# A four-layer graph network on one core: attention projections inside the attention passes, zero products, and a shorter path between passes

## The reference

```python
x = _layernorm(x + gcn(x, edge_weight))       # two convolutions with relu, then x @ Wfc + bfc
x = _layernorm(x + gat(x))                    # 8 heads
x = _layernorm(x + hgt(x, node_type, edge_type))
x = _layernorm(x + l3(x))

# gat, after its own layer norm and x @ W_in + b_in
e = leaky(scores_u[src] + scores_v[dst]); ex = exp(e - segment_max(e, dst)[dst])
agg = segment_sum(x[src] * ex, dst) / segment_sum(ex, dst)
out = agg @ W_ff + b_ff

# hgt: k, q, v by node type, kt and vt by edge type
e = (q[dst] * kt).sum(-1) * pri * scale; a = softmax of e over the edges of dst
agg = segment_sum(a * vt, dst)
out = relu(agg @ W_a[node_type] + x @ loop_weight + bias)   # W_a[type] = sum of 4 basis matrices, scaled

# l3
e = relu([h_src, h_dst] @ V.T + b) + h_src @ D.T + h_dst @ E.T; out = segment_sum(xw[dst] * scaler * e, src)
```

## Time and profile before

| | us |
|---|---|
| median of 3 runs | 7790.5 |
| the profiled execution | 7788.46 |
| its span | 7786.7 |
| PE busy in the span | 5059.6 (65%) |
| DVE busy | 4681.0 (60%) |
| ACT busy | 3283.5 (42%) |
| POOL busy | 4933.0 (63%) |
| indirect DMAs: sort, four passes, l3 | 784, 3328, 832 |
| data moved | 921.29 MB, 118 GB/s |

### The profile page before, as it was taken

One profiled execution on the slowest core, in us unless ns is written; L12 is line 12 of the kernel. 1 busy time (PEld: TensorE's weight loads), 2 busy tenths in 40 slices (PEclk: granted clock), 3 DMA queues, 4 the chain that ended last, 5 costly groups with the idle time before them and its releaser, 6 DMA issues. The chain is left out here.

```text
span 7786.7 us, 118192 instructions
## 1 busy us (share of the span) xinstructions
PE 5059.6 (65%) x26286; PEld 3803.4 (49%) x26287; DVE 4681.0 (60%) x12672; ACT 3283.5 (42%) x7820; POOL 4933.0 (63%) x4975
## 2 busy tenths in 40 slices
PE   6777775666665677772555557865666665777774
PEld 4555654444454555551444444435555543555553
DVE  7666664555554777774445545436666566566666
ACT  0222221444444455440444434435666541655553
POOL 0677775777776777774777770037777700777774
PEclk6666566888887888885666668977877777898897
DMA  0222221222223122233666672457777722666665
GB/s 27 59 53 54 55 55 46 54 55 55 55 55 47 53 55 54 55 52 90 179 180 179 182 164 85 143 169 221 234 225 229 216 69 80 208 201 200 201 200 139
DMA packets 818177, 921.29 MB, mean 118 GB/s; under 512 B 120930, under 2 KB 657002, under 8 KB 817706
## 3 DMA queue, kind: packets, MB, share of 16 engines
q0 software_dynamic: 198144, 441.54, 22.6%
q1 hardware_dynamic: 403498, 368.52, 15.9%
q10 hardware_dynamic: 216320, 109.07, 4.8%
HBM read 724.85 MB, written 193.87 MB: 118 GB/s over the span
## 5 line engine op out<-in xcount | busy, mean ns | idle before, releaser
L783 POOL DMA_INDIRECT arena<-t,stage_idx x3328 | 3268.1, 982 | 1249.8 <-issue 992.8
L822 PE MATMUL ps<-arena 128*128 128x128 f32 (+2 forms) x8320 | 1801.7, 378 | 770.0 <-DMA arena<-t,stage_idx 640.3
L822 PEld LDWEIGHTS ps<-arena 128*128 128x128 f32 x8320 | 1581.2, 258 | 1036.3 <-issue 935.6
L831 DVE TENSOR_TENSOR arena<-arena,ps 128x512 f32 (+2 forms) x1040 | 835.2, 803 | 733.0 <-PE ps L822 666.9
L739 POOL DMA_INDIRECT d_rec<-arena x784 | 782.5, 998 | 438.7 <-issue 241.5
L2664 POOL DMA_INDIRECT arena<-t,stage_idx x832 | 831.7, 1000 | 297.0 <-issue 224.2
L819 PE MATMUL ps<-int_tmp 128*128 128x512 bf16 (+1 forms) x1664 | 554.5, 402 | 622.9 <-DVE arena L831 340.3
L1861 PE MATMUL ps<-arena 128*128 x2496 | 393.4, 295 | 584.5 <-DVE arena L2087 323.5
L1263 PE MATMUL ps<-arena 128*128 128x416 f16 x3328 | 721.5, 368 | 0.0
L1195 ACT ACTIVATE arena<-arena 128x128 f16<-128x128 f16 x1664 | 662.2, 480 | 6.9
L1861 PEld LDWEIGHTS ps<-arena 128*128 128x128 f32 (+1 forms) x2496 | 346.6, 204 | 642.1 <-issue 620.9
(11 more groups left out here) (445 smaller groups left out, 8254.2 us busy)
## 6 DMA issues: line engine op xcount, KB each, us to landing
spill<-arena ACTq DMA_DIRECT2D x208, 512.0 KB
arena<-spill SPq DMA_DIRECT2D x208, 512.0 KB
arena<-t,stage_idx POOLq DMA_INDIRECT x4160
arena<-d_loT SPq DMA_DIRECT2D x208, 256.0 KB
arena<-s_loT SPq DMA_DIRECT2D x104, 512.0 KB, 4.8
arena<-key_d SPq DMA_DIRECT2D x98, 512.0 KB
t<-arena SPq DMA_DIRECT2D x98, 512.0 KB, 3.0
d_rec<-arena POOLq DMA_INDIRECT x784
```

Of the source, the lines that this page charges most:

```text
L783: pool.indirect_dma_start(out=rows[r][:, i, :], out_offset=None, in_=table, in_offset=bass.IndirectOffsetOnAxis(ap=stage_idx[:, 8 * r + i: ...
L822: return nc.tensor.matmul(self.banks[i // 4][:, bass.ds(self.slot[i], self.width)], weights, rows, start=False, stop=False, skip_group_che ...
L831: nc.vector.tensor_tensor(at, at, got, ALU.add).then_inc(self.added, 1)
```

## The change

Nine parts, line numbers in the order rows below being those of the changed program:

1. Load: SP loads the edges and x; ACT issues the 29 other loads. Four semaphores take the place of one, and the cast waits for the 12 loads of the edges.
2. Histogram: 32 products of zeros (bf16, 128x512) ahead and 2 behind each step's counts.
3. Tables: SP stores 4 of the 7 tiles of a group, ACT 3.
4. `clear_slowly`: before a clear of half z, `times` fp32 products of zeros with 512 columns into that half's bank. Per step: c1 2 (half 0), c2 1 (half 0), gat 2 in each half, hgt none, l3 1 (half 0). They stand ahead of the wait for the gathered rows or messages. None in the attention passes' tails.
5. The decode stage is gone; its operations run between the steps of c2's node tail, its stores at the end.
6. gat's projection, bias, residual and norm (`ThirdNodes`) run in gat's pass, hgt's output (`FourthNodes`) in hgt's: one tile in two steps, from step 24 on, in three and in six or seven vector steps for the four tiles left in the tail. The look-up uses one set of banks in place of two: in hgt the second half's look-up stands behind the first half's `weigh`, and waits for VectorE to have read the first; VectorE multiplies and reduces half by half. The first four windows are written out.
7. n3 keeps a copy of x, its transposes, the typed and the row products.
8. n4 keeps a copy of x, transposes, hidden products, row products and VectorE's row operations; the rows are double-buffered, the W products stand ahead of the row products.
9. n5: the last three stores are issued by ACT.

```diff
+                def zero_products(times):
+                    for _ in range(times):
+                        nc.tensor.matmul(bank(6).rearrange("p (r f) -> p r f", f=P), zeros16[:, 0:P], bcast_mid(zeros16[:, 0:P], 4), start=True, stop=True)
+                zero_products(32)
...
                         last.then_inc(free, 1)
+                        zero_products(2)
...
-                dve.wait_ge(loads, n_all)
+                dve.wait_ge(edges_in, 16 * 12)
...
+            def clear_slowly(self, z, times):
+
+                for _ in range(times):
+                    wide = self.banks[z][:, 0:512].rearrange("p (r f) -> p r f", f=P)
+                    nc.tensor.matmul(wide, zeros32, bcast_mid(zeros32, 4), start=True, stop=False, skip_group_check=True)
+                self.clear(z)
...
-                    for i, number in enumerate(numbers(sp, GT * k, GT)):
+                    for i, number in enumerate(numbers(sp, GT * k, BY_SP)):
...
+        SPARE = {"c1": 2, "c2": 1, "gat": 2, "hgt": 0, "l3": 1}
...
-                                sums.clear(z)
+                                sums.clear_slowly(z, (1 - z) * SPARE[which])
...
                 for s in range(self.TAIL, self.TAIL + self.STEPS):
                     self.vector_step(dve, s, self.in_tail(s, (0, 3, 5, 7, 9, 10)))
+                    self.decoded(dve, s - self.TAIL)
...
+            def scalar(self, act, m, b):
+                at = ((1, m),) if b else ((4, m - 2), (2, m - 1), (0, m))
+                self.scalar_step(act, 2 * m + b, [(h, t, 1) for h, t in at if underway(t)])
...
+                        nc.scalar.activation(x2T, self.features_bank(w), ACT.Copy)
+                        for i in range(w):
+                            for q in range(NB):
+                                last = nc.scalar.activation(As[:, (NB * i + q) * D:(NB * i + q + 1) * D], A[:, D * i:D * (i + 1)], ACT.Copy,
+                                                            scale=node_c[:, bass.ds(4 * NB * (t + i) + 3 * NB + q, 1)])
...
+        def attention_pass(which, idx, table, width, keep, tab, tab_w, head_last, Nodes):
...
-                        sums.clear(s)
+                        sums.clear_slowly(s, weigh.spare)
...
+                        if not gat:
+                            looked(n, b, 1)
...
+                        need(pe, v_s, 2 * n - 1 if gat else 2 * n + z)
...
-        attention_pass("hgt", d_typed, t3, 2 * D, D, q_tab, D, False)
+        attention_pass("hgt", d_typed, t3, 2 * D, D, q_tab, D, False, FourthNodes)
...
+        both_rows = [scratch(o, GT * R5).rearrange("p (t f) -> p t f", f=R5) for o in (TYPED_AT, AT_ACC)]
...
+                        if i == 0:
+                            need(pe, v_r, ROWS_V * (k - 1) + GT + 1)
+                            products(x3T, W_T, 4).then_inc(w_ps, 1)
                         nc.tensor.matmul(rows_bank(i), hT[:, i * P:(i + 1) * P], VDE, start=True, stop=True).then_inc(vde_ps, 1)
+                        if more and i == 2:
+                            transposed(k + 1)
+                        if more and i == 4:
+                            hidden(k + 1)
```

More of the change, by code:

```diff
@@ L237, in _ @@
[L237 to L243, removed]
+                    sp.dma_start(dst[:, 0:full, :], t[name][0:full * P * EC].rearrange("(j p e) -> p j e", p=P, e=EC)).then_inc(edges_in, 16)
@@ L1687, in windows, with node_step, node_step_behind @@
             def windows(eng, body):
-                body(0)
-                body(1)
-                with eng.Fori(2, WINDOWS) as w:
+                for w in range(4):
                     body(w)
+                with eng.Fori(4, WINDOWS) as w:
+                    body(w)
+            nodes = Nodes(sums, exp_ps)
+            def node_step(of, eng, w, j):
+                of(eng, 4 * w - nodes.FIRST_HALF // 2 + j // 2, j % 2)
+            def node_step_behind(of, eng, j):
+                if j >= 3:
+                    of(eng, 4 * WINDOWS - nodes.FIRST_HALF // 2 + (j - 3) // 2, (j - 3) % 2)
             def live(w):
@@ L2513, in turn @@
                     assert step.n == ROWS_V, step.n
-                ahead(dve, first, turn)
             @block.tensor
             def _(pe):
-                def add_row(name, b):
-                    for i in range(GT):
-                        last = nc.tensor.matmul(ps[:, b * 512 + i * D:b * 512 + (i + 1) * D], ones[0:1, :], bias[name][0:1, :], start=False, stop=True, skip_group_check=True)
-                    return last
-                def start(k):
-                    pe.wait_ge(a_rdy, k + 1)
-                    transposes(A, 0).then_inc(t_ps, 1)
-                    pe.wait_ge(t_sb, 2 * k + 1)
-                    pe.wait_ge(xs_in, k + 1)
-                    transposes(xs, 0).then_inc(t_ps, 1)
@@ L2547, in turn, with transposed, hidden @@
-                def turn(k, more):
-                    if more:
-                        start(k + 1)
-                        need(pe, v_r, ROWS_V * k)
-                        for i in range(EARLY):
-                            typed(k + 1, i)
-                        pe.wait_ge(t_sb, 2 * k + 4)
+                def transposed(k):
                     pe.wait_ge(x_rdy, k + 1)
                     transposes(x_new, 0).then_inc(xt_ps, 1)
-                    if more:
-                        for i in range(EARLY, 5):
-                            typed(k + 1, i)
+                def hidden(k):
@@ L2559, in turn, with first @@
                     pe.wait_ge(xt_sb, k + 1)
-                    products_T(U_T, x3T, 0).then_inc(h_ps, 1)
-                    if more:
-                        for i in range(5, GT):
-                            typed(k + 1, i)
-                        pe.wait_ge(summed, SUMS * (GT * k + 2 * GT))
-                    else:
-                        pe.wait_ge(v_r, ROWS_V * k)
+                    products_T(U_T, x3T, 2).then_inc(h_ps, 1)
+                def first(k):
+                    transposed(k)
+                    hidden(k)
@@ L2567, in turn @@
+                def turn(k, more):
                     pe.wait_ge(h_sb, k + 1)
```

678 lines of the change are left out of this document (429 added, 249 removed).

## The result

The changed kernel takes 7908.91 us (median of 4 runs, 7903.22 to 7917.36), the kernel before 7792.74 beside it: a ratio of 1.0152, 95% interval 1.0139 to 1.0165, 118 us slower. I had forecast 7643 us, faster with a chance of 0.92. The profiled execution has a span of 7911.0 us against 7786.7.

What follows compares the result with a forecast made beforehand. GpSimd's scatters and gathers were taken to set the pace, about 10.3 us a step, so gains lay only outside its queue; terms summed to -147.5 us, a median of 7643, range 7590 to 7730.

Steps and rivals of the forecast that it cites:

- The view of the bound: All passes: GpSimd's gathers set the pace, about 10.3 us a step; other engines' work must fit within that.
- HGT's output, inside the pass: Output work moved from n4 into hgt's pass: +5 us for the gathers, +42 in the tail, net -115 with n4.
- rival B: hgt's pass: steps outgrow GpSimd through node work and the single look-up bank, +54 us, 7697; chance 0.14.
- The tails: Behind the last gathers of gat and hgt: node work for the four tiles left adds +22 and +42 us.
- n4 and n3: Stages after hgt and gat: work moved out into the passes shortens them by 157 and 29 us.
- Load: Load stage: with the weights on ACT's queue and separate semaphores the cast starts when the edges have landed, -10 us.
- decode: Between c2 and gat: the separate stage goes, its DVE work moves into c2's node tail, -12.5 us.
- The histogram: Histogram stage: at full clock zero products and counts fit beneath DVE's 1.28 us a step, waits for PE go, -12 us.
- Rival A: Histogram: PE stays at half clock despite the zero products, +12 +66 us, 7721; chance 0.15.
- The fills: Zero products in c1, c2 and l3: they run in PE's idle time while GpSimd ends every step, 0 us.
- C: Both attention passes: gathers lengthen beside more DVE work, +45 us less the 10 counted, 7678; chance 0.04.
- D: gat's pass: fills at half clock make PE's step outgrow 10.3 us, +468 us, 8111; chance 0.05.

Runs made afterwards that it cites:

- hgt_multiply_first_b: Changed kernel with both hgt look-ups in a row on TensorE and VectorE's first multiply ahead of the lagging messages: 7902.68 us, ratio 1.0146 to the kernel before.

## Why the prediction was wrong

*The view of the bound* was right: GpSimd sets the pace of every pass, before and after, as long as a step of the other engines stays under 10.3 us; a higher clock there gave nothing.

*HGT's output, inside the pass*, is the step that failed: I put +5 for the gathers and named rival B at +54 with a chance of 0.14. It came to +214, 2.1 us a step. B's mechanism is what happened: a step of the other engines outgrew GpSimd's eight gathers. Its price failed, in two places.

The larger is the node work. I set 1.7 us of it on VectorE against a room of 1.6 as if only its busy time counted, and nothing for the waits that it brings. Taken out, the gathers are back at 1085.6 us. With two banks, where the look-up's wait is nearly gone (11.9 us), VectorE's and ScalarE's part of it alone costs 81 to 86 us, while VectorE still waits 121.3 us for gathers (238.0 before, over the whole pass): the room was not used up, and yet the steps grew. The rows of hgt_multiply_first_b show one reason, node steps of three engines that wait for each other. Another may be that the room is partly spent on the pauses that VectorE has at the end of a window of eight steps (4.4 to 5.0 us ahead of L775 in the changed kernel, 3.2 to 5.2 before). Both are read from traces; the run that was to test the first stayed open.

The smaller is the look-up. "A wait for PE of 0.4 a step may double": it became 2.3, since doubling counts neither the whole second look-up (1.66 us in the step shown) nor the clear and four products (2.02 us for the products) put ahead of it, though part 6 of the change names that order. But this wait alone costs little: without node work it is 251.1 us and the gathers grow by 7 to 12. What it costs together with the whole node work is inside the 120 us that the runs do not divide. (B's "about 0.6 a step" is 1.7 + 0.4 - 1.6 = 0.5 by its own terms; that is not what missed.)

*The tails* were undersized: +37.5 and +59 against +22 and +42. In gat's tail each tile's step costs VectorE some 3.4 us (4741.94 to 4745.38) among the last lagging steps, and TensorE's four products behind it take 2.02 us in place of 1.09, at a granted clock that falls from 1.00 (4680 to 4700) to 0.66 (4700 to 4720) and is 0.84 from 4740 to 4760. In hgt's tail VectorE waits 18.4 us for the products of the last four tiles, of which three take 2.08 us for eight records and only the first less.

*n4 and n3* were right: -150 and -30.3 against -157 and -29. The largest term of the sum held. *Load* -13.3 (-10), *stores* -6.6 (-4.5) and *decode* -10.1 (-12.5) held as well.

*The histogram* gave nothing against -12. The open point that I named went my way: the clock is 1.00 from 40 to 170, up from 0.50. What failed was the next step, that VectorE's 13.4 us of waits for TensorE would go and its step shrink to 1.28 us: I had put the fills beneath it at no cost. VectorE, then TensorE:

```profile
59.65 20.61 DVE L343 TENSOR_TENSOR arena<-arena 128x392 bf16<-128x392 bf16 x46
```

```profile
59.74 0.33 PE L475 MATMUL ps<-arena 128*128 128x392 bf16 x1
59.91 0.91 PE L477 MATMUL ps<-arena 128*128 128x49 bf16 x8
60.63 0.61 PE L459 MATMUL ps<-int_tmp 128*128 128x512 bf16 x2
61.08 0.33 PE L475 MATMUL ps<-arena 128*128 128x392 bf16 x1
```

VectorE still takes 1.34 us a step, what it took before, and the stage from the end of the load to the first scatter is as long as it was (190.9 and 191.6 us). TensorE now has no idle time between its products: the counts take 0.89 us (59.74 to 60.63) and the two products of zeros (L459) 0.45, together 1.34. The next step's counts start only behind them, and VectorE still waits: each of its steps starts 0.16 to 0.18 us after the end of TensorE's counts for the buffer that it needs (0.16 to 0.20 before), and ahead of it VectorE stands idle 0.09 to 0.14 us, too short for the timeline to print. Where it need not wait, in the stage's first steps, its three operations start 0.27, 0.27 and 0.60 us apart, some 1.15 a step. So what the clock gave, the fills took back. This is read from the rows; no run left them out. Rival A, the half clock, did not come.

*The fills* cost 21 us where I had 0. *C* (longer gathers) and *D* (gat at half clock) did not come: gat's PE is busy 825 of 1192 us at 0.80, and a gather lasts 996 ns in hgt and 1008 in l3, 8 to 9 more than before.

## What to carry to other kernels

The time that an engine off the critical path waits for the pacing engine is room only for work that brings no waits of its own. Before moving work into a pass, walk one step of every engine in the new order, with each semaphore it takes, and look for a place where all of them meet. Here the move took 150 us out of n4 and put 214 and 59 into hgt's pass and its tail. When a bank is shared to make space, count what now stands between the two uses, not the use itself. And price a higher clock only in stretches that TensorE ends, less the time of the products that raise it.

## What the runs showed of the hardware

Products of zeros do raise the granted clock: 0.50 to 1.00 in the histogram with 32 bf16 products of 512 columns ahead and two in each step, and in gat 0.65 to 0.80 with four fp32 ones a step. That removes what I had left open about zeros. The Trainium skill (TensorE: Matmul & The Clock Gate, Part 1), by which activity releases a throttled clock, agrees with that.

The kernel before took 7776 to 7801 us in some series and 9673 to 9816 in others. The four long series ran on three chips and the two short ones on two other chips, so it may be a matter of the chip. GpSimd's DMAs last as long in both (0.97 to 1.02 us in the passes), and with the changed load stage the time to the first scatter is the same (214 to 217 us); the added time is in sort and the passes (the sort's scatters took 1367 to 1385 us against 1030 to 1035); in c1 VectorE and ScalarE stand still for 13 to 16 us at a time. In a long series the fills cost 296 us and not 21. That it is the fetching of instructions is my guess; no run tested it, and in c1 the pauses come twice in a turn of the loop, so not only at its end.
